# A transformer block on one core: the value product of a group of heads moved half a period earlier

## The reference

```
x = x + 0.5 * moe(layernorm(x))
x = x + attention(layernorm(x))
x = x + 0.5 * moe(layernorm(x))

attention:  16 heads of width 8; scores = q k^T / sqrt(8) - slope_h * (key - query), causal
            out = softmax(scores) v ; out @ Wo^T
moe:        8 experts (top 2 of a softmax router) and a gated shared expert,
            each 128 -> 128 -> 128
```

## Time and profile before

| | us |
|---|---|
| median of 3 runs | 318.75 (316.54 to 320.65) |
| the profiled execution | 317.94 |
| its span | 316.2 |
| TensorE busy | 286.5 (91%) |
| VectorE busy | 251.3 (79%) |
| ScalarE busy | 175.6 (56%) |
| GpSimd busy | 127.7 (40%) |
| attention stage, first to last transposed score | 97.5 to 241.7 us of the span |
| mean granted clock of TensorE | 0.968 |

### The profile page before, as it was taken

The page is one execution under the profiler, slowest core; times in us unless marked ns, Lnnn a source line. Parts: engine busy times, 40 slices in busy tenths (PEclk is TensorE's granted clock), DMA queues, the critical chain, the costliest instruction groups (busy, mean ns, idle before and its releaser), DMA issues.

```text
span 316.2 us, 7140 instructions
## 1 busy us (share of the span) xinstructions
PE 286.5 (91%) x2328; PEld 185.6 (59%) x2328; DVE 251.3 (79%) x1039; ACT 175.6 (56%) x342; POOL 127.7 (40%) x251
## 2 busy tenths in 40 slices
PE   0889998999998898999799999999999999999994
PEld 0688886977664343334433344333443799989994
DVE  3799898889787787998778989998621698988875
ACT  2423433433555777878578888886888333334330
POOL 1355256306128623575324534666533352420200
PEclk9999999999997599999889999997999999999999
DMA  6910000660022113411113411110000001000011
GB/s 169 244 24 2 0 0 4 224 167 11 3 101 100 42 51 116 151 54 53 51 40 127 140 54 52 54 55 1 4 2 2 0 3 33 2 18 20 1 32 35
DMA packets 20668, 17.73 MB, mean 56 GB/s; under 512 B 2460, under 2 KB 19420, under 8 KB 20572
## 3 DMA queue, kind: packets, MB, share of 16 engines
q1 hardware_dynamic: 19912, 17.05, 18.0%
q10 hardware_dynamic: 720, 0.23, 0.4%
HBM read 9.74 MB, written 7.34 MB: 54 GB/s over the span
## 4 chain that ended last, share of the span: by engine, by line
PE 61%; DVE 14%; POOL 9%; issue 8%; ACT 4%; DMA 2%; SPq 1%; DVEq 0%; POOLq 0%
PE bank L904 16%; PE bank L1033 10%; PE bank L1001 8%; PE bank L839 6%; PE bank L841 5%; PE bank L840 5%; DVE X L699 4%; POOL probs L402 3%; DVE masked_s L767 2%; PE bank L974 2%; DMA X<-in_x 2%; DVE stats L622 2%; PE bank L1043 2%; ACT probs L528 2%; PE bank L1056 2%
## 5 line engine op out<-in xcount | busy, mean ns | idle before, releaser
L767 DVE CUSTOM_DVE_ANT_0 masked_s<-bank,causal_sb 128x512 f32<-128x512 f32 (+3 forms) x256 | 110.0, 486 | 16.0 <-PE bank L974 15.8
L528 ACT ACTIVATE probs<-bank 128x512 f32<-128x512 f32 x160 | 89.7, 602 | 26.0 <-PE bank L1001 25.1
L699 DVE SCALAR_TENSOR_TENSOR X<-bank,coef,X 128x128 f32<-128x128 f32 x272 | 76.2, 342 | 16.2 <-PE bank L904 13.2
L904 PEld LDWEIGHTS bank<-w_sb,act 128*128 128x128 f32 x512 | 67.3, 192 | 6.6 <-ACT act L451 1.1
L904 PE MATMUL bank<-w_sb,act 128*128 128x128 f32 x512 | 67.7, 275 | 0.6 <-ACT act L451 0.6
L402 POOL TENSOR_SCALAR_AFFINE_SELECT probs<-probs 128x512 f32<-128x512 f32 x64 | 39.8, 635 | 65.5 <-ACT probs L528 65.5
L974 PE MATMUL bank<-KA,QA 54*128 54x512 bf16 (+3 forms) x256 | 59.0, 318 | 4.8 <-DVE smax L767 4.1
L451 ACT ACTIVATE act<-bank 128x512 f32<-128x512 f32 x72 | 41.7, 594 | 37.3 <-PE bank L841 36.7
L1001 PE MATMUL bank<-QA,KA 57*128 57x128 bf16 (+3 forms) x256 | 59.3, 317 | 0.9 <-issue 0.7
L1033 PE MATMUL bank<-probs,VA 128*32 128x256 f32 (+2 forms) x640 | 53.6, 403 | 1.4 <-issue 0.9
L839 PE MATMUL bank<-XH,w_hi 128*128 128x512 f32 x88 | 42.3, 481 | 3.0 <-DVE gated L684 1.8
(11 more groups left out here) (87 smaller groups left out, 334.4 us busy)
## 6 DMA issues: line engine op xcount, KB each, us to landing
qk_scratch<-qk_parts SPq DMA_DIRECT2D x8, 384.0 KB, 2.6
QA<-qk_scratch SPq DMA_DIRECT2D x32, 96.0 KB, 2.2
KA<-qk_scratch SPq DMA_DIRECT2D x32, 96.0 KB, 2.3
qk_scratch<-qk_parts SPq DMA_DIRECT2D x8, 256.0 KB, 2.9
qk_scratch<-qk_parts SPq DMA_DIRECT2D x8, 128.0 KB, 2.8
QA<-smaxT SPq DMA_DIRECT2D x64, 3.0 KB
out_x<-X SPq DMA_DIRECT2D x4, 256.0 KB, 2.3
X<-in_x SPq DMA_DIRECT2D x3, 256.0 KB, 6.1
```

The lines of the kernel that those rows point to most:

```text
L528: nc.scalar.activation(dst, src, ACT.Exp).then_inc(exp_done, 1)
L699: m = nc.vector.scalar_tensor_tensor(X[:, b * NT + t, :], Y_BANK[i % 3][:, t * P:(t + 1) * P], coef[:, j % 2, t, n:n + 1], X[:, b * NT + t ...
L767: r = nc.vector.tensor_tensor_reduce(masked_s[:, u % 4, off:off + n], bank[:, off:off + n], causal_sb[:, S - n:S], 1.0, -3e38, ALU.add, AL ...
L904: m = nc.tensor.matmul(Y_BANK[i % 3][:, r], a, w2_sb[:, n, :], start=True, stop=True)
```

## The change

The value product of group n begins in its own period: pieces 0 and 1 at slots 7 and 8 of period n, pieces 2, 3 and 4 at slots 0, 1 and 3 of period n + 1. Its copy stands behind exponential 4, its transposition at slot 6 and its normalisation at slot 7 (of VectorE's loop) of period n + 1. The maxima are transposed at slot 4 instead of 3 and copied behind exponential 5 instead of 3. The projections stand at slot 2 instead of 4, and what reads them moves too. `batch_done` comes a period sooner (n = 4, 8, 12, 16), so the last batch's attention output is transposed in period 16, and its product with Wo follows combine 1 of `ffn(1)`.

```diff
-        OUT_SLOT = 7
+        OUT_SLOT = 6
-        XT_TAIL = ((NGT - 2, 4), (NGT - 1, 3))
+        XT_TAIL = ((NGT - 2, 2), (NGT - 1, 2))
         def batch_done(n):
-            b, rest = divmod(n - 5, NG)
+            b, rest = divmod(n - 4, NG)
...
 ScalarE
-                        if n == 3 and j == B:
-                            copy_at(B - 1)
...
-                    if i == 3 and 0 <= n + 1 < NGT:
+                    if i == 4 and 0 <= n - 1 < NGT:
+                        copy_out(n - 1)
+                    if i == 5 and 0 <= n + 1 < NGT:
                         copy_smax(n + 1)
...
-                            if i == 5:
+                            if i == 3:
                                 high_qk(b, k)
-                            if i == 7:
+                            if i == 6:
                                 middle_qk(b, k)
...
-                if 0 <= n - 1 < NGT:
-                    copy_out(n - 1)
 VectorE
-                        if j == B and n == 0:
-                            normalise(NGT - 1)
-                        if j == B and n == 5:
+                        if j == B and n == 2:
                             add_attention(B - 1)
...
-                    if i == OUT_SLOT and 0 <= n - 2 < NGT:
-                        normalise(n - 2)
+                    if i == OUT_SLOT + 1 and 0 <= n - 1 < NGT:
+                        normalise(n - 1)
...
-                        if (b := projected_at(n, 2 + k)) is not None and i == 5:
+                        if (b := projected_at(n, 2 + k)) is not None and i == 4:
                             rest_qk(b, k)
 TensorE
-                            if n == 0:
-                                transpose_out(NGT - 1)
-                            if n == 2:
-                                transpose_ao(B - 1)
-                            if n == 4:
+                            if n == 1:
                                 output(B - 1)
...
-            PIECE_SLOTS = (2, 3, 5, 6, 8)
+            EARLY_PIECES, LATE_PIECES = {7: 0, 8: 1}, {0: 2, 1: 3, 3: 4}
...
-                    if i == 3 and 0 <= n + 1 < NGT:
+                    if i in LATE_PIECES and 0 <= n - 1 < NGT:
+                        weigh_values(n - 1, LATE_PIECES[i])
+                    if i == 4 and 0 <= n + 1 < NGT:
                         transpose_smax(n + 1)
-                    if i == OUT_SLOT and 0 <= n - 2 < NGT:
-                        transpose_out(n - 2)
-                    if i in PIECE_SLOTS and 0 <= n - 1 < NGT:
-                        weigh_values(n - 1, PIECE_SLOTS.index(i))
+                    if i == OUT_SLOT and 0 <= n - 1 < NGT:
+                        transpose_out(n - 1)
+                    if i in EARLY_PIECES and 0 <= n < NGT:
+                        weigh_values(n, EARLY_PIECES[i])
...
-                    if (b := projected_at(n, 2)) is not None and i == 4:
+                    if (b := projected_at(n, 2)) is not None and i == 2:
                         project(b, 0)
-                    if (b := projected_at(n, 3)) is not None and i == 4:
+                    if (b := projected_at(n, 3)) is not None and i == 2:
                         project(b, 1)
```

## The result

The change makes the kernel slower: 356.25 us median against 319.21, a ratio of 1.122 (95% interval 1.116 to 1.128), +37.0 us. (Some executions of a kernel take longer at a lower granted clock; medians take in all executions, ratios only the others.) The profiled execution has a span of 355.2 us.

The account below looks back on a forecast made before the run. The maxima's round trip was taken to bound the loop: 1.8 + 7.7 + 9.8 + 0.9 + 1.6 + 1.5 + 1.8 - 0.8 + 1.7 = +26.0 on 317.94, so 344 us, range 334 to 354.

Parts of the forecast that it names:

- The trip as the bound: Attention loop: from the maxima's copy start to the next period's first score takes 4.44 us; plain periods become 9.2 to 9.8.
- the wait for the transfer: First score of a period waiting for the maxima to land: in nearly every period, from 1.6 to some 15 to 25 us.
- The wait at the bank behind a projection: Periods 1, 2, 6, 7: the maxima's transposition waits 1.6 us for VectorE's remainder; periods 12.0 each, +9.8 us in all.
- One fall more, +1.7: TensorE's clock falls once more, costing 1.7 us, half of 3.5 us at 1.2 GHz as in periods 6 and 7.
- The end: -0.8: Periods 15 and 16 lose two pieces (1.14) and a transposition (0.6), but gain 0.9 of wait: -0.8 us.
- The 0.9 us set down for the wait of the last batch's transposition: Period 16: the last output's normalisation and copy have little TensorE work beside them, 0.9 us of wait.
- The waits for masks go: Later value pieces remove TensorE's 3.1 us of mask waits and 3.7 for split maxima; no credit, already inside the loop's 9.5.
- The floor: Rival: the loop is the bound but ScalarE and the bank cost nothing, 327 to 334 us; chance 0.15.
- the covered landing: Rival: the maxima's transfer stays covered, copy within 4.7 us of the first score; nothing changes, 317 to 323 us; chance 0.08.
- the gain: Rival: copy early enough, mask and split-maxima waits and two end pieces go, no bank wait; 310 us; chance 0.07.
- The third rival: The clock falls in eight of fifteen periods at 1.7 us on top of the forecast's 24: 354 to 366 us; chance 0.10.
- The rule cited for it: A transfer wait in each loop turn can return every turn to the slow clock; sum some 12 us higher.

Follow-up runs that it names:

- Experiments 1 to 3: 1: kernel before, maxima's copy moved in eleven periods, 326.50 us; 2: changed kernel, ScalarE issues two of four transfers, 346.29 us; 3: changed kernel, maxima's copy first, 337.72 us.
- experiment 3: Changed kernel with ScalarE copying the maxima ahead of the product's copy, both behind exponential 4: 337.72 us median, ratio 1.047 to the kernel before.

## Why the prediction was right about the waits and wrong about the clock

Forecast: 344 us with a range of 334 to 354, 26.0 more than before. Measured: 356.25, 37.0 more, above that range. By stretch, in us:

| stretch | before | forecast | changed | changed, waits filled |
|---|---|---|---|---|
| period 0 | 11.6 | 12.5 | 12.6 | 12.6 |
| 1 and 2 | 18.6 | 24.0 | 30.0 | 24.1 |
| 3 | 7.7 | 9.5 | 9.4 | 10.8 |
| 4 and 5 | 19.7 | 21.3 | 21.4 | 21.4 |
| 6 and 7 | 19.6 | 24.0 | 24.9 | 23.3 |
| 8 | 9.3 | 10.7 | 11.0 | 11.1 |
| 9 to 12 | 31.4 | 39.1 | 38.2 | 38.6 |
| 13 and 14 | 19.4 | 21.2 | 20.2 | 20.1 |
| 15 to the end | 81.6 | 80.8 | 89.3 | 83.0 |

The forecast's 1.7 us for the clock stands in none of these rows. The cut at 234.65 us in the earlier trace rows is late: TensorE's row of four scores at 234.19 already holds the first of period 15, so the last row before is some 0.45 us more and the one above it as much less.

- **The trip as the bound: right for the plain periods.** Forecast a copy at 4.8 to 5.2 us, a trip of 4.44, plain periods of 9.2 to 9.8; measured 4.85, 4.46 and 9.31. Experiments 1 to 3 move the copy or the trip and the plain periods follow. But the wait for the transfer was to be in nearly every period, and it is in nine; the trip does not end periods 1, 2, 4, 6, 7 and 8.
- **The wait at the bank behind a projection: right.** 1.6 us in each of four periods was forecast and 6.4 us in four waits measured. With the waits filled and the clock up, the two pairs take 24.06 and 23.32 us against 24.0 each.
- **"One fall more, +1.7": this is the step that failed.** The term was mis-sized. Filling the waits gives back 10.9 us (356.25 to 345.33), and with them filled the increase is 26.5 us (345.33 - 318.81), against 24.3 for all terms of the forecast but the clock. The forecast counted one more fall, as short as the one in periods 6 and 7 of the kernel before (3.5 us at half clock). From the clock shares of the rows, an estimate: from period 1 on the kernel before was at half clock for some 10 us, the changed one for some 50, of which 19.5 at a stretch (0.50 from 265 to 284.5 us). The price of a microsecond at half clock was not set too low; how often and how long was.
- **"The end: -0.8": wrong, +7.7 measured** (some +7.3 by the right cut), and mostly for the same reason. With the waits filled it is +1.5, and with the copy first (experiment 3), where the clock did not fall, +0.7. The 0.9 us set down for the wait of the last batch's transposition was about right (0.77, with the waits filled 1.09); the rest of the way from -0.8 to these numbers is not accounted for.
- **What the forecast did not name**: the output's transposition waiting for the maxima's copy at the bank, 16.6 us. In a plain period it stands in the same uncovered stretch as the wait for the transfer (1.33 and 1.00 us, the period being copy plus trip all the same), so it should cost little there by itself; no run takes it out alone. This, and the six periods that other work ends, would be why the wait for the transfer grew to 8.8 us only, and not to the 15 to 25 forecast.
- **"The waits for masks go": wrong.** They are 4.5 us in 14 waits, 3.1 before; those for split maxima are nearly gone (0.9 us once, 3.7 in eight before).
- **The rivals.** The floor (no wait at the bank) and the covered landing are out by the rows above; so is the gain, whose point, a copy within 4.7 us, was missed by 0.15. The third rival, falls in most periods on top of the forecast, has the time measured in its range (354 to 366), yet came true by another way: plain periods kept the full clock, and the loss sits in periods 1, 2, 6, 7 and 14 to 16. The rule cited for it (the Trainium skill, TensorE: Matmul & The Clock Gate, HAM oscillation) comes from a loop that waits some 3 to 5 us for a transfer in each turn. Read as the prediction read it, it would have a fall in every turn here; the trace has 1.00 over periods 9 to 12, each of which ends on a wait for the transfer of 0.41 to 1.00 us. A neighbouring section of that page of the Trainium skill (A second HAM failure mode: psum-queue depth-cycling) tells of a kernel in which frequent short idle stretches between groups of matmuls suffice to make the clock go up and down. Periods 1 and 2 agree, with a clock of 0.67 and these waits, while the 1.33 and 1.00 us of periods 10 to 12 did not bring a fall:

```profile
116.71 0.38 PE L979 MATMUL bank<-id_b,smax 128*12 128x128 bf16 x4 [1.59 <-DVE qk_rest L738]
...
118.66 1.09 PE L1035 MATMUL bank<-id_f,OT 128*128 128x128 f32 x4 [0.82 <-ACT smaxT L532]
```

- **The idle stretch ahead of a fall in the kernel before.** The prediction read "hardly more than 1 us" from the slice 153 to 154. TensorE's row behind it has 1.50 us, near the 1.59 of the four periods with a projection, whose clock was down as well. The fall of periods 13 and 14 there (0.91) has no such row: the longest wait of a matmul in the six microseconds ahead is 0.57.

```profile
154.49 0.63 PE L1050 MATMUL bank<-id_f,AO 128*128 128x128 f32 x4 [1.50 <-DVE XL L630]
```

Open: which waits bring a fall, and why the clock came back within four microseconds in some places and only after more than nineteen at the end. Shown is what filling the waits gives back, and that most of the falls go with it.

## What to carry to other kernels

Where a transfer goes once round in every turn of a loop, write down its whole way (what must be done before it starts, its own time, who waits for it): moving its start by two slots added nothing to TensorE's busy time and 1.7 us in the mean to a plain turn (31.38 to 38.20 us over four). A bank that several steps share is a second queue; look at who is next in it after each move. And when a change puts short waits into TensorE's stream, price the clock apart from the waits: here filling them gave back 11 us of 37.

## What the runs showed of the hardware that was not expected

- Where the next first score follows the landing, four transfers of 3 KB from one queue take 4.44 to 4.46 us from the start of the copy ahead of them to that matmul, in over twenty periods of these traces (4.39 to 4.41 in periods 13 and 14); two on each of two queues 3.3 to 3.65.
- A kernel can get faster by doing more: with 111 more matmul instructions (2439 for 2328) in TensorE's waits the changed kernel took 10.9 us less, and the granted clock rose from 0.905 to 0.975.
